# A batch's softmax weights applied by one VectorE product instead of four scalings, in both cross attentions

## The chip, the cores and the metric

The kernel runs on one core of one Trainium2 chip. The metric is the device time of one execution in microseconds (us), the median of several runs.

## The reference

A two-layer perceiver-like block on x of shape 32 batches x 32 tokens x 512. Each layer is a cross attention to a context (32 x 257 x 128), then a self attention, then a feed-forward stage (dense in layer 0, mixture of experts in layer 1). The change touches the two cross attentions alone (L0x and L1x in the program's names). Cut to the part that matters, one of them computes

```python
q_r = jnp.einsum('bshq,hqr->bhsr', q_big, W_qr)
k_r = jnp.einsum('bld,hdr->bhlr', kv_rope, W_kr)
scores = jnp.einsum('bhsr,bhlr->bhsl', q_r, k_r)
attn = jax.nn.softmax(scores, axis=-1)
ctx_c = jnp.einsum('bhsl,bld->bhsd', attn, kv_rope)
ctx_lat = jnp.einsum('bhsd,hkd->bshk', ctx_c, w_kc_kv)
out = ctx_lat.reshape(b, s, H * K) @ Wo.T
```

for 16 heads. The softmax goes over 257 context rows; the kernel subtracts the last context row from all others beforehand, so that 256 scores remain and the last one's exponent is a term of its own (the "tail").

## The kernel before, in words

Work is cut by batch. A batch has 32 tokens x 16 heads = 512 query rows, which stand as 4 groups of 128 partitions with 256 scores each. So a batch's exponents are one tile `prob` of 128 x (4 x 256) floats, of which three are used in turn. The order on every engine is written out by hand: `tensor_attention`, `scalar_attention`, `vector_attention` and `pool_attention` are loops over b, and each engine works through its own loop in order; semaphores couple them.

In one pass of its loop each engine does the following.

- TensorE (PE): turns the keys of batch b+1 (`turn_keys`, L463, L464), scores batch b (L477), mixes batch b-3 with its probabilities (`mix`, L98), turns the probabilities of batch b-2 (`turn_probs`, L490), and from b = 7 on projects a quarter of a token tile out (`project_out`, L98). For b below 7 it folds one head's output weights instead (L455).
- ScalarE (ACT): four exponentials of batch b, one for each group, which also write their sums (L573), and the tail's (L575); then the high parts of the turned probabilities of b-2 (L537), the mixed context of b-3 (L553), the high part of a projection's operand (L549), the next keys (L563).
- VectorE (DVE): the low part of a projection's operand (`split_lo`, L618), the row maxima of batch b (`find_peak`, L627, L630), then `weigh` for batch b-1, the low parts of the turned probabilities of b-2 (L595). After every fourth projection it adds the finished tile to x (L606) and takes its statistics (L149, L151, L153).
- GpSimd (POOL): rotates the context rows of batch b+2 (`rotate_keys`, L415, L418, L419, L421, L423), splits those of b-2 into high and low parts (L399, L401). After every fourth projection it stands in its queue at the root of the variance of that tile (`next_root`, L159), which waits for DVE's statistics.

`weigh` adds the tail to the four sums (L635), takes the reciprocals (L637), and then scales the four groups of `prob` in place, each by its own column of reciprocals (L640). `turn_probs` on PE waits until the sixth step of the batch is counted.

What follows `weigh` in DVE's queue is L595; what waits for its result is `turn_probs` one pass later.

Of the kernel before, what the change touches and what calls it, by code (L numbers as in the profile page):

```python
# [7 lines left out]
ALU = mybir.AluOpType  # L8
# [6 lines left out]
P = 128  # L15
BANK = 512
B, S, D = 32, 32, 512
# [5 lines left out]
LC = (L - 1) // P  # L23
# [49 lines left out]
class Signals:  # L73
# [5 lines left out]
    def take(self, name, total):  # L79
        if name not in self.sems:  # L80
            self.sems[name] = self.ctx.enter_context(self.nc.semaphore(f"s_{name}"))
        base = self.total.get(name, 0)
        self.total[name] = base + total
        return Signal(self.sems[name], base)
# [151 lines left out]
class LatentAttention(Stage):  # L236
# [15 lines left out]
    def sb(self, n, shape, dt=F32, arena=None):  # L252
        return (arena or self.arena).enter_context(self.sh.nc.sbuf_tensor(f"{self.name}_{n}", shape, dt))
# [5 lines left out]
    def attention_memory(self):  # L259
        sb, take, sh = self.sb, self.take, self.sh  # L260
        self.craw = [sb(f"craw{i}", [P, 3, DC]) for i in range(2)]
        self.rot = sb("rot", [P, 3, DC])
        self.kcos, self.ksin = sb("kcos", [P, 3, DC]), sb("ksin", [P, 3, DC])
        self.kv = [sb(f"kv{i}", [P, 3, DC]) for i in range(5)]
        self.kvT = [sb(f"kvT{i}", [P, LC * P + S]) for i in range(self.NKT)]
        self.prob = [sb(f"prob{i}", [P, 4, LC * P]) for i in range(3)]
        self.pT = [tuple(sb(f"pT_{v}{i}", [P, LC, BANK], F32R) for v in ("hi", "lo")) for i in range(2)]
        self.kvs = [tuple(sb(f"kvs_{v}{i}", [P, LC, DC], F32R) for v in ("hi", "lo")) for i in range(2)]
        self.small = [sb(f"small4_{i}", [P, 5, 4]) for i in range(4)]
        self.wn = tuple(sb(f"wn_{v}", [P, XH, D], F32R) for v in ("hi", "lo"))  # L270

        self.part_hi = [sb(f"part_hi{i}", [P, BANK], F32R) for i in range(2)]
        self.s_bank = [sh.psum(i) for i in range(3)]
        self.o_bank, self.t_bank, self.c_bank, self.k_bank = sh.psum(3), sh.psum(4, 2), sh.psum(6), sh.psum(7)
        self.c_landed = [take(f"c_landed{i}", 48 * B // 2) for i in range(2)]
        self.tabs_landed = take("rope_landed", 32)
        self.folded = take("folded", XH)
        self.wn_hi, self.wn_lo = take("wn_set", XH), take("norm_sum", XH)
        self.q_back = take("expert_landed2", 16 * self.HALF)
        self.part_hi_set, self.part_lo_set = take("copied", BPT * NT), take("squared", BPT * NT)  # L280
        self.rope = take("rope", 5 * B)
        self.kT_made = take("kT_made", B)
        self.kT_set = take("kT_set", B)
        self.scored = take("scored", 2 * B)
        self.peak = take("peak", 3 * B)
        self.exped = take("exped", 5 * B)
        self.weighed = take("weighed", 6 * B)
        self.prob_turned = take("prob_turned", 2 * B)
        self.pT_hi = take("pT_hi", 2 * B)
        self.pT_lo = take("pT_lo", 2 * B)  # L290
        self.kv_split = take("kv_split", 2 * B)
        self.mixed = take("mixed", B)
        self.ctx_set = take("ctx_set", B)
        self.projected = take("projected", BPT * NT)
        self.x_set = take("x_set", NT)
        self.ends = [(self.x_set, NT)]

        self.mixed_all = [(self.x_set, NT - 1), (self.ctx_set, B), (self.kT_set, B)]
        self.out_w = [sh.add_weights(sh.d[f"{self.name}_out"][n], OUT_HEADS * OUT_PACK, [(self.folded, OUT_HEADS * (n + 1))])
                      for n in range(XH // OUT_HEADS)]  # L300
# [180 lines left out]
    def turn_probs(self, pe, b):  # L481
        src = self.prob[b % 3]
        if b == 0:
            self.folds_kept(pe, self.FIRST)
        pe.wait_ge(self.weighed, 6 * b + 6)
        pe.wait_ge(self.pT_hi, 2 * b)
        pe.wait_ge(self.pT_lo, 2 * b)
        for c in range(LC):
            for r in range(4):
                ins = pe.e.transpose(self.t_bank[:, c * BANK + r * P:c * BANK + (r + 1) * P], src[:, r, c * P:(c + 1) * P],  # L490
                                     self.sh.ident[:])
            ins.then_inc(self.prob_turned.sem, 1)
# [128 lines left out]
    def find_peak(self, dve, b):  # L621
        mx, neg = (self.small[b % 4][:, n, :] for n in range(2))
        for g in range(2):
            bank = self.s_bank[(2 * b + g) % 3]
            dve.wait_ge(self.scored, 2 * b + g + 1)
            dve.wait_ge(self.weighed, 6 * (b - 3))
            dve.e.tensor_reduce(mx[:, 2 * g:2 * g + 2], bank.rearrange("p (r n) -> p r n", r=2), AX_X,  # L627
                                ALU.max).then_inc(self.peak.sem, 1)
        dve.wait_ge(self.peak, 3 * b + 2)
        dve.e.tensor_scalar(neg, mx, -1.0, 0.0, ALU.mult, ALU.min).then_inc(self.peak.sem, 1)  # L630

    def weigh(self, dve, b):
        dst, (sums, tail, rec) = self.prob[b % 3], (self.small[b % 4][:, n, :] for n in (2, 3, 4))
        dve.wait_ge(self.exped, 5 * b + 5)
        dve.e.tensor_tensor(sums, sums, tail, ALU.add).then_inc(self.weighed.sem, 1)  # L635
        dve.wait_ge(self.weighed, 6 * b + 1)
        dve.e.reciprocal(rec, sums).then_inc(self.weighed.sem, 1)  # L637
        dve.wait_ge(self.weighed, 6 * b + 2)
        for r in range(4):
            dve.e.tensor_scalar(dst[:, r, :], dst[:, r, :], rec[:, r:r + 1], None, ALU.mult).then_inc(self.weighed.sem, 1)  # L640


class FoldedQueries(LatentAttention):
# [2455 lines left out]
```

## Time and profile before

| | |
|---|---|
| median of 3 runs | 2112.19 us |
| lowest and highest | 2111.12, 2112.3 us |
| span of the profiled execution (first to last instruction) | 2106.8 us |
| PE busy | 1996.1 us (95%) |
| DVE busy | 1203.5 us (57%) |
| POOL busy | 972.1 us (46%) |
| mean granted TensorE clock | 0.985 |

The profiled execution's own device time isn't given beside its span; the median's 2112.19 us stands 5.4 us above the span. The first cross attention's loop over batches lies between about 125 and 385 us of the span, the second's between about 1114 and 1380 us. PE's matmuls are pipelined and their ends are modelled: a row's duration overlaps the next one's start, so gaps in the starts say more than durations.

### The profile page before, as it was taken

To read this page: it belongs to the slowest core of one execution; us is meant where nothing else is said; L and a number is where in the kernel's file an instruction comes from. 1 tells how busy PE (TensorE), PEld (TensorE's weight loads), DVE (VectorE), ACT (ScalarE), POOL (GpSimd) and SP (SyncE) were. 2 spreads that over 40 slices of the span, in tenths; PEclk is the share of its full clock that TensorE was granted. 3 is DMA by queue.
4 is the path that set the end of the run, shared out by engine and by line. 5 is a ranking of instruction groups with operands and counts; after the bars stand their busy time and mean duration, and the time that the engine had idled before them with its cause. 6 is when DMAs were issued, how large, how long until landed. Compare 5 with 4: busy or idle time off the path is not lost. (4 is left out here: it accounts for less than half of the span.)

```text
span 2106.8 us, 28714 instructions
## 1 busy us (share of the span) xinstructions
PE 1996.1 (95%) x9018; PEld 1421.9 (67%) x9018; DVE 1203.5 (57%) x2739; ACT 898.1 (43%) x2115; POOL 972.1 (46%) x928
## 2 busy tenths in 40 slices
PE   7989999998999999999998999979978999999997
PEld 6868888776688744666656888767655555555553
DVE  4368998567551022555547899779863443444444
ACT  2356666334422100333335666635524444454542
POOL 1266684211352100676768666476203444555552
PEclk9999999999999999999999999989988999999999
DMA  5421221200311100111222121110345999989887
GB/s 209 150 100 42 58 58 37 82 1 1 120 42 52 35 1 0 52 57 61 70 107 66 43 67 43 66 67 1 110 148 154 312 298 327 210 213 221 209 218 186
DMA packets 103411, 226.29 MB, mean 107 GB/s; under 512 B 14288, under 2 KB 56784, under 8 KB 94768
## 3 DMA queue, kind: packets, MB, share of 16 engines
q1 hardware_dynamic: 80688, 170.85, 24.0%
q0 software_dynamic: 21136, 51.11, 11.9%
q10 hardware_dynamic: 1440, 2.49, 0.3%
q8 instruction: 77, 1.26, 0.2%
q14 instruction: 70, 0.57, 0.1%
HBM read 266.86 MB, written 42.48 MB: 147 GB/s over the span
## 5 line engine op out<-in xcount | busy, mean ns | idle before, releaser
L98 PE MATMUL banks<-L1f_w,L1f_xT 128*128 x760 | 265.1, 492 | 1.9 <-issue 1.3
L2872 POOL DMA_INDIRECT moe_sums<-L1f_y,L1f_row x94 | 149.3, 1589 | 219.5 <-DVE L1f_is_who L2739 162.2
L159 POOL TENSOR_TENSOR rstd<-rstd,power 128x1 f32<-128x1 f32 x48 | 35.4, 738 | 361.1 <-DVE rstd L153 361.1
L98 PEld LDWEIGHTS banks<-L1f_w,L1f_xT 128*128 128x128 f32 x760 | 138.0, 192 | 82.0 <-issue 6.8
L2690 DVE SCALAR_TENSOR_TENSOR L1f_z<-banks,L1f_share,L1f_sg 128x192 f32<-128x192 f32 x95 | 39.7, 418 | 147.8 <-ACT L1f_sg L2623 147.7
L2880 POOL DMA_INDIRECT L1f_xg<-moe_rows,L1f_row x95 | 94.2, 991 | 61.5 <-DVE L1f_spare L2730 24.6
L2623 ACT ACTIVATE L1f_sg<-banks 128x192 f32<-128x192 f32 x95 | 31.4, 331 | 206.9 <-PE banks L98 145.5
L98 PE MATMUL banks<-L0f_down,L0f_z 128*128 128x512 f32 x256 | 111.1, 592 | 1.5 <-DVE L0f_z L2147 1.5
L98 PE MATMUL banks<-L0f_hT_hi,L0f_ug_hi 128*128 128x512 f32 x256 | 100.0, 391 | 0.0
L98 PE MATMUL banks<-L0f_hT_hi,L0f_ug_lo 128*128 128x512 f32 x256 | 99.6, 389 | 0.0
L98 PE MATMUL banks<-L0f_hT_lo,L0f_ug_hi 128*128 128x512 f32 x256 | 99.6, 389 | 0.0
L2600 PE MATMUL banks<-L1f_w,L1f_zT 128*128 x190 | 97.3, 594 | 1.8 <-ACT L1f_zT L2632 1.8
L2601 PE MATMUL banks<-L1f_w,L1f_zT 128*128 x190 | 97.0, 592 | 0.0
L2219 POOL TENSOR_TENSOR L0f_ug_lo<-w,L0f_ug_hi 128x512 fp32r<-128x512 f32 x32 | 42.9, 1353 | 113.2 <-ACT L0f_ug_hi L2123 113.2
L573 ACT ACTIVATE L1x_prob<-banks,L1x_small 128x256 f32<-128x256 f32 x128 | 59.0, 473 | 82.3 <-DVE L1x_small L630 82.3
L573 ACT ACTIVATE L0x_prob<-banks,L0x_small 128x256 f32<-128x256 f32 x128 | 59.0, 473 | 80.7 <-DVE L0x_small L630 80.7
L1115 PE MATMUL banks<-L1x_y,L1x_u 128*128 128x512 f32 x192 | 87.7, 593 | 1.6 <-ACT L1x_u L1165 0.9
L98 PEld LDWEIGHTS banks<-L0f_down,L0f_z 128*128 128x128 f32 x256 | 48.1, 190 | 59.7 <-issue 59.7
L2729 DVE TENSOR_SCALAR L1f_row_f<-L1f_found 128x1 f32<-128x1 f32 x95 | 14.6, 154 | 128.6 <-ACT L1f_sign L2664 127.3
L2147 DVE SCALAR_TENSOR_TENSOR L0f_z<-banks,L0f_su,L0f_sg 128x1024 f32<-128x1024 f32 x16 | 20.5, 1283 | 109.8 <-PE banks L98 109.8
L1242 POOL TENSOR_TENSOR xn<-xn,L1x_sinq 128x512 f32<-128x512 f32 x32 | 41.6, 1299 | 76.0 <-ACT xn L1141 76.0
L1246 POOL TENSOR_TENSOR L1x_y<-L1x_y,L1x_turn_part 128x1024 f32<-128x1024 f32 x32 | 75.7, 2365 | 0.0
(425 smaller groups left out, 5672.5 us busy)
## 6 DMA issues: line engine op xcount, KB each, us to landing
L1f_w<-in_experts SPq DMA_DIRECT2D x95, 1280.0 KB
L1f_laid<-moe_counts SPq DMA_DIRECT2D x59, 512.0 KB
w<-in_L1x_heads SPq DMA_DIRECT2D x16, 704.0 KB, 4.1
w<-in_L0x_heads SPq DMA_DIRECT2D x8, 1216.0 KB, 5.7
w<-in_wug SPq DMA_DIRECT2D x8, 1024.0 KB, 4.9
L0x_craw<-in_ctx SPq DMA_DIRECT2D x96, 64.0 KB, 2.9
L1x_craw<-in_ctx SPq DMA_DIRECT2D x96, 64.0 KB, 2.2
w<-in_L0x_out SPq DMA_DIRECT2D x4, 1280.0 KB, 5.5
```

What stands on the lines that cost most here:

```text
L98: ins = pe.e.matmul(out, w, m, start=first and n == 0, stop=last and n == len(pairs) - 1)
L159: pool.e.tensor_tensor(self.rstd[:, i:i + 1], self.rstd[:, i:i + 1], self.power[:, 0:1], ALU.pow).then_inc(self.rstd_set.sem, 1)
L573: act.e.activation(dst[:, r, :], bank[:, (r % 2) * 256:(r % 2 + 1) * 256], ACT.Exp, bias=neg[:, r:r + 1], accum_out=sums[:, r:r + 1]).then ...
L1115: ins = pe.e.matmul(self.sh.psum(self.SMALL), self.u[h % 2][:, c, :], self.y[k % 3][:, c, :], start=c == 0, stop=c == QC - 1)
L1242: pool.e.tensor_tensor(self.by_tile(buf[:], 1), self.by_tile(buf[:], 1), self.table(self.sinq[:, 2:3], 1), ALU.mult).then_inc(self.rest_si ...
L1246: pool.e.tensor_tensor(y[:, 0:2], y[:, 0:2], self.turn_part[k % 2][:], ALU.add).then_inc(self.pair_set.sem, 1)
L2219: pool.e.tensor_tensor(lo[:], self.ug_source(n), hi[:], ALU.subtract).then_inc(self.ug_lo.sem, 1)
L2600: pe.e.matmul(out, zT[:, 0, :], self.weights(slot, self.GU, at), start=True, stop=False)
L2601: pe.e.matmul(out, zT[:, 1, :], self.weights(slot, at, at + D), start=False, stop=True).then_inc(self.y_made.sem, 1)
L2690: dve.e.scalar_tensor_tensor(out=self.z[j % 2][:], in0=self.gu_bank(j)[:, EI:2 * EI], scalar=self.share[:, j:j + 1], in1=self.sg[j % 2][:] ...
L2872: pool.e.indirect_dma_start(self.sums[j % 2][:, :], bass.IndirectOffsetOnAxis(ap=self.row[:, j:j + 1], axis=0), self.y[j % self.NY][:], No ...
L2880: pool.e.indirect_dma_start(self.xg[j % self.NX][:], None, self.rows_of[:, :], bass.IndirectOffsetOnAxis(ap=self.row[:, j:j + 1], axis=0)) ...
```

## The change

The four scalings become one product of the whole tile with the four reciprocals, each repeated 256 times by a stride of zero. The semaphore `weighed` counts three steps a batch instead of six.

```diff
-        self.weighed = take("weighed", 6 * B)
+        self.weighed = take("weighed", 3 * B)
@@ turn_probs
-        pe.wait_ge(self.weighed, 6 * b + 6)
+        pe.wait_ge(self.weighed, 3 * b + 3)
@@ find_peak
-            dve.wait_ge(self.weighed, 6 * (b - 3))
+            dve.wait_ge(self.weighed, 3 * (b - 3))
@@ weigh
         dve.wait_ge(self.exped, 5 * b + 5)
         dve.e.tensor_tensor(sums, sums, tail, ALU.add).then_inc(self.weighed.sem, 1)
-        dve.wait_ge(self.weighed, 6 * b + 1)
+        dve.wait_ge(self.weighed, 3 * b + 1)
         dve.e.reciprocal(rec, sums).then_inc(self.weighed.sem, 1)
-        dve.wait_ge(self.weighed, 6 * b + 2)
-        for r in range(4):
-            dve.e.tensor_scalar(dst[:, r, :], dst[:, r, :], rec[:, r:r + 1], None, ALU.mult).then_inc(self.weighed.sem, 1)
+        dve.wait_ge(self.weighed, 3 * b + 2)
+        dve.e.tensor_tensor(dst[:], dst[:], rec.rearrange("p (r o) -> p r o", o=1).to_broadcast([P, 4, LC * P]),
+                            ALU.mult).then_inc(self.weighed.sem, 1)
```

## Rows read from the trace of the kernel before

**Rows 1.** The page's first part: busy us, share of the span and instructions of each engine.

```profile
PE 1996.1 (95%) x9018; PEld 1421.9 (67%) x9018; DVE 1203.5 (57%) x2739; ACT 898.1 (43%) x2115; POOL 972.1 (46%) x928
```

**Rows 2.** Busy time by stretch: length, PE, PEld, DVE, ACT, POOL, clock, DMA share, GB/s.

```profile
200.00:300.00 100.00, 99.85 (x486) 84.97 (x486) 91.58 (x171) 63.42 (x182) 73.90 (x97) 1.00 0.27 70
...
1200.00:1300.00 100.00, 99.85 (x489) 84.80 (x488) 90.40 (x168) 63.27 (x182) 73.42 (x98) 1.00 0.23 60
```

**Rows 3.** Timeline of PE: start us, us, engine, line. One L464 for each batch.

```profile
251.59 0.24 PE L464 MATMUL banks<-ident,L0x_kv 32*128 32x32 f32 x1
...
259.23 0.24 PE L464 MATMUL banks<-ident,L0x_kv 32*128 32x32 f32 x1
...
267.19 0.24 PE L464 MATMUL banks<-ident,L0x_kv 32*128 32x32 f32 x1
```

**Rows 4.** Timelines of DVE, POOL and PEld after the first tile's last projection.

```profile
198.26 0.69 DVE L606 TENSOR_TENSOR x<-x,banks 128x512 f32<-128x512 f32 x1 [0.28 <-PE banks L98]
...
200.16 0.92 POOL L159 TENSOR_TENSOR rstd<-rstd,power 128x1 f32<-128x1 f32 x1 [11.90 <-DVE rstd L153]
...
202.04 0.59 POOL L418 TENSOR_TENSOR L0x_rot<-L0x_craw,L0x_ksin 128x192 f32<-128x192 f32 x1
...
202.42 2.89 DVE L640 TENSOR_SCALAR L0x_prob<-L0x_prob,L0x_small 128x256 f32<-128x256 f32 x4
...
202.59 0.64 POOL L419 TENSOR_TENSOR L0x_rot<-L0x_craw,L0x_ksin 128x192 f32<-128x192 f32 x1
...
203.31 1.02 POOL L421 TENSOR_TENSOR L0x_kv<-L0x_kv,L0x_rot 128x384 f32<-128x384 f32 x1
...
204.41 0.74 POOL L423 TENSOR_TENSOR L0x_kv<-L0x_kv 128x256 f32<-128x256 f32 x1
...
205.44 0.37 PEld L463 LDWEIGHTS banks<-ident,L0x_kv 128*128 128x128 f32 x2
```

**Rows 5.** Timelines of DVE and PEld at the second and third tile's end.

```profile
229.09 0.68 DVE L606 TENSOR_TENSOR x<-x,banks 128x512 f32<-128x512 f32 x1
...
236.01 0.20 PEld L463 LDWEIGHTS banks<-ident,L0x_kv 128*128 128x128 f32 x2 [0.21 <-POOL L0x_kv L423]
...
259.90 0.68 DVE L606 TENSOR_TENSOR x<-x,banks 128x512 f32<-128x512 f32 x1
...
266.82 0.20 PEld L463 LDWEIGHTS banks<-ident,L0x_kv 128*128 128x128 f32 x2 [0.57 <-POOL L0x_kv L423]
```

**Rows 6.** Timelines of DVE and POOL, where a DVE operation on two SBUF tiles meets POOL's.

```profile
245.47 1.00 POOL L421 TENSOR_TENSOR L0x_kv<-L0x_kv,L0x_rot 128x384 f32<-128x384 f32 x1
...
245.57 1.44 DVE L618 TENSOR_TENSOR L0x_ctx_lo<-L0x_qT,L0x_part_hi 128x512 fp32r<-128x512 f32 x1 [0.73 <-ACT L0x_part_hi L549]
...
246.55 1.06 POOL L423 TENSOR_TENSOR L0x_kv<-L0x_kv 128x256 f32<-128x256 f32 x1
...
1320.12 1.36 DVE L618 TENSOR_TENSOR L1x_ctx_lo<-L1x_qT,L1x_part_hi 128x512 fp32r<-128x512 f32 x1 [0.20 <-ACT L1x_part_hi L549]
...
1320.89 1.05 POOL L418 TENSOR_TENSOR L1x_rot<-L1x_craw,L1x_ksin 128x192 f32<-128x192 f32 x1
```

**Rows 7.** Groups by line and shape: busy us, mean ns | idle before.

```profile
L640 DVE TENSOR_SCALAR L0x_prob<-L0x_prob,L0x_small 128x256 f32<-128x256 f32 x128 | 70.5, 612 | 1.1
...
L1852 DVE TENSOR_TENSOR L1a_pr<-L1a_pr,L1a_tiny 128x512 f32<-128x512 f32 x8 | 5.5, 692 | 0.3
...
L1474 DVE TENSOR_TENSOR L0a_wq_lo<-w,L0a_wq_hi 128x2048 fp32r<-128x2048 f32 x1 | 2.3, 2284 | 0.0
```

**Rows 8.** One line's instructions: duration ns min/median/max, first and last start.

```profile
L423 POOL TENSOR_TENSOR L0x_kv<-L0x_kv x32: 724/737/1072, 61.8 to 338.2; 128x256 f32<-128x256 f32 x32
```

**Rows 9.** Timelines of DVE and PE, at the loop's start and at its end.

```profile
139.83 1.14 DVE L640 TENSOR_SCALAR L0x_prob<-L0x_prob,L0x_small 128x256 f32<-128x256 f32 x4
...
173.05 3.26 DVE L640 TENSOR_SCALAR L0x_prob<-L0x_prob,L0x_small 128x256 f32<-128x256 f32 x4
...
359.04 0.49 PE L98 MATMUL banks<-L0x_pT_hi,L0x_kvs_hi 128*128 128x512 f32 x1 [1.50 <-ACT L0x_qT L553]
```

## The prediction

> **What bounds the kernel now.** I read the page's busy shares first: PE has 95% of the span, DVE 57%, POOL 46% [rows 1]. That says where to look, not what a change is worth, so next comes busy time by stretch. In the two cross attentions PE is busy 99.85 of 100 us while DVE has 91.58 and 90.40 and POOL about 74 [rows 2]. The reader should see two things there: PE sets the pace, and DVE is close enough behind it that it could be a bound for a batch here and there. Third is the timeline of PE, with one L464 as a mark for each batch. From batch 8 on the marks stand 7.60 us apart, nearly without exception; the exception is a batch of 7.96 us (259.23 to 267.19, after 7.64 us from 251.59 to 259.23) [rows 3]. There are three batches of 7.96 us that start so, one in the first attention and two in the second. Each is the batch behind a finished token tile. So outside a few places PE's own work is the time, and the question becomes what PE waits for at those places.
>
> The answer is in the timelines of the other engines there. After every fourth projection DVE adds the tile to x (L606) and takes statistics, POOL stands idle for them (11.90 us at the first tile), takes the root (L159) and only then rotates the next keys, L415 to L423, and PE's next key turn (L463) waits for L423 [rows 4]. From L606's start at 198.26 to L423's end at 205.15 are 6.89 us; PE needs the keys at 205.44. So 0.29 us are left when L606 starts as soon as PE has finished the tile. When DVE comes late with L606 the keys are late: the second tile's L606 is at 229.09 where PE's rhythm (198.26 + 4 x 7.60 = 228.66) would have allowed 228.66, and the load waits 0.21 us, which PE's array doesn't feel (its period stays at 7.61); the third's is at 259.90, 0.8 us late, the load waits 0.57 us and the batch costs 0.36 us [rows 3, 5]. This happens five times in each attention (the sixth tile's end comes when no keys are left to rotate), ten in all; three cost 0.36 us, the others 0 to 0.02, 1.1 us together. **This chain DVE, POOL, PE is the only place in the steady part where something other than PE sets the time, and the change touches both of its engines.**
>
> **The change on DVE alone.** It removes four L640 a batch and adds one product. The four took 4 x 612 = 2448 ns of busy time on average, 64 batches, 157 us for both attentions [rows 7]. But undisturbed, four start and end within 1.14 us [rows 9]: they overlap in part, and the mean is made of waits. The trace has no product of 1024 columns from two SBUF tiles. Between a product with a repeated column on 512 columns at 692 ns and a difference of 2048 at 2284 ns [rows 7] lies (2284 - 692) / 1536 = 1.036 ns a column, so 692 + 512 x 1.036 = 1222 ns. Undisturbed, then, the new form is 0.08 us slower than the old one, not faster. From both sides: 1.14 us (nothing lost against four) to 2.28 us (as the row of twice the size).
>
> The Trainium skill, "VectorE: DVE Perf Modes", section "The perf-mode tier table", speaks against this change in the same way: a float32 scaling within SBUF runs at two elements a cycle, a product of two tensors at one. By its errata table (58 cycles + columns per mode at 0.96 GHz) four scalings would be 775 ns and the product 1127 ns, an estimate from that page, 0.35 us worse a batch; the rows above say 0.08. Neither sum needs it.
>
> **What the waits are.** DVE's L618, a difference of two SBUF tiles on 512 columns, starts at 245.57 within POOL's L421 (to 246.47) and ends at 247.01, that is 0.54 us behind L421's end; 512 columns at 1.036 ns are 0.53. So it stood until POOL's operation was over and then ran. POOL's next, L423, starts at 246.55 and takes 1.06 us where its usual is 0.74 [rows 6, 8]; it ends 0.60 us behind L618. The same at 1320: L618 ends at 1321.48, POOL's L418 takes 1.05 instead of 0.59 [rows 4, 6]. Operations of DVE and POOL that need the same way into SBUF exclude each other, one whole operation at a time, and the turn passes at the end of each. How the four scalings live with that shows at a tile's end: 202.42 to 205.31, 2.89 us for four, one in each gap between L418, L419, L421 and L423, and POOL loses next to nothing (0.64 instead of 0.59, 0.02 on L421) [rows 4].
>
> **The change where it matters: a tile's end.** The new product is issued at 202.42 like the first scaling. It gets the way when L418 ends at 202.63, holds it for 1024 x 1.036 = 1.06 us and ends at about 203.7. Then L419 runs: behind L618 the 192-column L418 ended 0.46 us after it (1321.94 against 1321.48) [rows 6], so L419 ends at 204.2 instead of 203.23. L421 and L423 follow without further loss, so L423 ends 0.94 us later than now (0.97 less the few hundredths that the scalings cost). PE's load comes 0.94 - 0.29 + 0.05 = 0.70 us late, of which 0.18 are hidden as rows 5 show (0.54 late cost 0.36). **Cost 0.52 us for each tile's end**, when L606 comes as early as PE allows. It should: a tile's end that costs PE something gives DVE and ACT that time to catch up (after the 0.36 us at 267 the next L606, at 289.88, again waited for PE), and DVE is freer. Ten ends: +5.2, less the 1.1 that they cost today: **+4.1 us**. Bounds: from 0 new (POOL held as little as by the scalings; -1.1) to 0.52 + 0.41 us at each (L606 as late as it is today, by 0.41 us on the mean of the ten: 9.3 - 1.1 = +8.2).
>
> **In the other batches of the steady part** DVE gets 4 scalings' 2.2 to 3.2 us down to 1.1 to 2.1 (own time and the rest of one POOL operation, at most 1.0). Hidden: PE has no wait there. POOL is held up to 1.06 us once a batch, of which it has room: 7.60 us a batch against 5.7 of work. The batch behind a tile's end is the tightest, 2.1 us between L423's end at 210.96 and PE's need at 213.04; two holds make 1.9, PE's own 0.5 comes to the good. I take 0.
>
> **At the loop's start.** For b = 3 to 6 the batches go round a ring DVE maxima, ACT exponentials, ACT L537, DVE L595, in which `weigh` isn't: nothing changes. In the batch at 173.05 the four take 3.26 us [rows 9] and L595 starts late behind them; PE's batch is 7.94 there instead of 7.60, in both attentions. The product would end by 175.2 and free L595, but POOL, itself held by the product of the batch before, delays L618 and the maxima. Between -0.34 and 0 each; I take -0.2, twice.
>
> **At the loop's end** PE waits 1.50 us for the mixed context (359.04) [rows 9], 1.46 in the second attention. That chain runs over ACT from the maxima of the last batches, which DVE could start up to 0.3 us earlier. I take -0.15, twice.
>
> The rest moves as it is: no transfer, no other wait of `weighed` is near (`turn_probs` comes a pass later).
>
> **Sum:** 4.1 - 0.4 - 0.3 = +3.4 us. On the span that is 2110.2 us; with the 5.4 us around it, which the median of the runs has over this span, **2115.6 us**. A measurement of this kernel tells 0.2%, 4.2 us, from no change; so this forecast is "no change", a little on the slow side.
>
> **Rivals.**
> 1. *Slower clearly: the hold is paid in full.* POOL's hold delays L618 and L630 in turn, so that L606 stays as late as now, and each tile's end pays 0.93 us, or the batch behind it pays as well. For it: L618 and L630 wait for POOL today (1.36 instead of 0.68 us), and POOL's slack behind a tile's end is 2.1 us. Against: PE's wait gives all others time. Price 8.2 - 0.7 = +7.5: 2119.7 us. It decides as soon as L606 starts more than 0.4 us behind PE's last projection.
> 2. *POOL isn't held.* The product reads one tile and a repeated column; if that leaves POOL its way, or POOL gets in between, only the relief of DVE stays: -1.1 for the tiles' ends, -0.7 and -0.6 for start and end: 2109.8 us. For it: no row has a repeated column beside POOL. Against: L618 in both directions.
> 3. *DVE is the hidden bound.* Its 91% and the coupling over ACT in the loop's first seven batches and at its end (PE waits of 1.0, 1.2, 0.9 and 0.4 us there, 1.5 at the end) could all shrink by half, 3 us in each attention: 2106.2 us. Against: the waits before L595 there end with ACT.
>
> **How the numbers follow.** Forecast 0.45, rival 1 0.25, rival 2 0.2, rival 3 0.1. Slower by over 0.2% (above 2116.4): all of rival 1 and about a quarter of the forecast, 0.36. Faster (below 2108.0): rival 3 and a little of rival 2, 0.12. Within: 0.52. The range takes rival 2's time and rival 1's: 2109.5 to 2120. The forecast's own range is 2113.5 to 2117.5, by the bounds at start and end and a tenth of a microsecond or two at each tile's end.
>
> **What the profile would show.** One L640 a batch, TENSOR_TENSOR, 1.2 us at least and up to 2.2, mean near 1.5; DVE's busy time down by about 55 to 60 us. At each of the ten tiles' ends POOL's L419 (or L418) at 1.5 us instead of 0.64, PEld L463 waiting about 0.7 us for POOL L423 instead of 0.21 or 0.57, and the period of PE's L464 at 8.1 us there. L606 led by PE at every end. Wrong if L419 stays at 0.6 us (rival 2), if the periods behind a tile's end are 8.5 us (rival 1), or if PE's waits in the first seven batches shrink (rival 3).

## The result, and the profile after

Median of 11 runs each: 2112.19 us before (2109.82 to 2115.22), 2117.12 us after (2113.95 to 2120.03). The ratio is 1.0020, 95% interval 1.0012 to 1.0029: 4.9 us slower. The two medians alone divide to 1.0023, just beyond the 0.2% that the prediction took as the smallest difference that tells; the interval lies above 1 and has 0.2% within it, so that the change costs time is clear of the noise, and that it costs more than 0.2% is not. Forecast were 2115.6 us, +3.4.

The page after, span and busy line, to be held against [rows 1]:

```profile
span 2115.2 us, 28522 instructions
PE 1999.5 (95%) x9018; PEld 1422.0 (67%) x9018; DVE 1151.2 (54%) x2547; ACT 899.5 (43%) x2115; POOL 1019.8 (48%) x928
```

DVE issues 192 instructions fewer (64 batches by three) and is busy 52.3 us less. POOL has the same 928 instructions and is busy 47.7 us *more*: an operation that is held is counted as busy. The two sums are nearly equal, and neither says yet what PE pays.

Busy time by stretch, the two stretches of [rows 2] (us, PE, PEld, DVE, ACT, POOL, clock, DMA share, GB/s):

```profile
200.00:300.00 100.00, 98.59 (x479) 83.46 (x478) 76.37 (x133) 63.62 (x182) 80.50 (x92) 1.00 0.26 68
1200.00:1300.00 100.00, 98.28 (x477) 82.96 (x476) 75.73 (x129) 63.35 (x182) 83.94 (x96) 1.00 0.22 59
```

DVE falls from 91 to 76 of 100 us, and PE, which sets the time, falls too, from 99.85 to 98.59 and 98.28. PE loses that at the ends of the token tiles. The timeline of PE where [rows 3] stood; after one ordinary period of 7.60 us comes one of 8.13 us behind the finished tile:

```profile
254.85 0.24 PE L464 MATMUL banks<-ident,L0x_kv 32*128 32x32 f32 x1
262.45 0.24 PE L464 MATMUL banks<-ident,L0x_kv 32*128 32x32 f32 x1
270.58 0.24 PE L464 MATMUL banks<-ident,L0x_kv 32*128 32x32 f32 x1
```

Before that, at the first tile's end, the timelines of DVE, POOL and PEld, for [rows 4]:

```profile
200.49 0.68 DVE L606 TENSOR_TENSOR x<-x,banks 128x512 f32<-128x512 f32 x1
...
202.38 0.93 POOL L159 TENSOR_TENSOR rstd<-rstd,power 128x1 f32<-128x1 f32 x1 [12.37 <-DVE rstd L153]
...
204.25 0.59 POOL L418 TENSOR_TENSOR L0x_rot<-L0x_craw,L0x_ksin 128x192 f32<-128x192 f32 x1
...
204.63 1.30 DVE L639 TENSOR_TENSOR L0x_prob<-L0x_prob,L0x_small 128x1024 f32<-128x1024 f32 x1
...
204.81 1.58 POOL L419 TENSOR_TENSOR L0x_rot<-L0x_craw,L0x_ksin 128x192 f32<-128x192 f32 x1
206.47 1.02 POOL L421 TENSOR_TENSOR L0x_kv<-L0x_kv,L0x_rot 128x384 f32<-128x384 f32 x1
207.57 0.73 POOL L423 TENSOR_TENSOR L0x_kv<-L0x_kv 128x256 f32<-128x256 f32 x1
...
208.35 0.20 PEld L463 LDWEIGHTS banks<-ident,L0x_kv 128*128 128x128 f32 x2 [1.19 <-POOL L0x_kv L423]
```

The product is issued while L418 still runs (to 204.84) and ends at 205.93. The 192 columns of L419, 0.64 us in [rows 4], take 1.58 us and end 0.46 us behind it. L421 and L423 follow without further loss. At the second and third tile (DVE and PEld, for [rows 5]):

```profile
231.41 0.69 DVE L606 TENSOR_TENSOR x<-x,banks 128x512 f32<-128x512 f32 x1 [0.21 <-PE banks L98]
...
239.28 0.20 PEld L463 LDWEIGHTS banks<-ident,L0x_kv 128*128 128x128 f32 x2 [0.74 <-POOL L0x_kv L423]
...
262.34 0.69 DVE L606 TENSOR_TENSOR x<-x,banks 128x512 f32<-128x512 f32 x1 [0.22 <-PE banks L98]
...
270.21 0.20 PEld L463 LDWEIGHTS banks<-ident,L0x_kv 128*128 128x128 f32 x2 [0.74 <-POOL L0x_kv L423]
```

At these two L606 starts as soon as PE is through, and the load of the keys still waits 0.74 us for POOL, where it waited 0.21 and 0.57 us. The product as a group (line and shape: busy us, mean ns | idle before), and as one line's instructions (ns min/median/max, first and last start), for [rows 7]; below it L419's, whose maximum was 1039 ns in the first attention before:

```profile
L639 DVE TENSOR_TENSOR L1x_prob<-L1x_prob,L1x_small 128x1024 f32<-128x1024 f32 x32 | 47.8, 1493 | 1.1
L639 DVE TENSOR_TENSOR L0x_prob<-L0x_prob,L0x_small 128x1024 f32<-128x1024 f32 x32 | 46.2, 1443 | 1.1
...
L639 DVE TENSOR_TENSOR L0x_prob<-L0x_prob,L0x_small x32: 1224/1298/1899, 137.3 to 364.7; 128x1024 f32<-128x1024 f32 x32
L639 DVE TENSOR_TENSOR L1x_prob<-L1x_prob,L1x_small x32: 1224/1554/1895, 1129.0 to 1357.8; 128x1024 f32<-128x1024 f32 x32
...
L419 POOL TENSOR_TENSOR L0x_rot<-L0x_craw,L0x_ksin x32: 584/596/1584, 61.4 to 341.7; 128x192 f32<-128x192 f32 x32
```

And PE's wait at the first attention's loop end (1.50 us in [rows 9]):

```profile
363.33 0.50 PE L98 MATMUL banks<-L0x_pT_hi,L0x_kvs_hi 128*128 128x512 f32 x1 [1.31 <-ACT L0x_qT L553]
```

**The account, from PE's L464 marks.** The period of batch 8 and those of the tile ends, in us; all others from batch 8 on are 7.56 to 7.64. The last column runs from the second of the 32 marks to the last:

| kernel | attention | batch 8 | ends of tiles 1 to 5 | second to last mark |
|---|---|---|---|---|
| before | first | 7.94 | 7.60, 7.61, 7.96, 7.60, 7.61 | 216.72 |
| before | second | 7.95 | 7.60, 7.62, 7.59, 7.97, 7.96 | 219.91 |
| after | first | 7.60 | 8.59, 8.13, 8.13, 8.14, 8.13 | 219.80 |
| after | second | 8.06 | 8.59, 8.13, 8.13, 8.14, 8.13 | 222.37 |

The loops are longer by 3.08 and 2.46 us, 5.5 together. The ten tile ends cost 2 x (0.99 + 4 x 0.53) = 6.2 us instead of 1.1, so +5.1; batch 8 gives 0.34 back in the first attention and costs 0.11 in the second, -0.2. The 0.7 us that are left lie ahead of batch 8 of the first attention (the eight periods there are 48.76 us before, 49.46 after). They can't be put down to the change: two profiles of one and the same kernel, the one with the product and the late root below, have 48.39 and 49.47 us there. The loops' ends give back 0.19 and 0.15 (from 1.50 and 1.46 us of wait to 1.31 and 1.31). What the marks give to the change is 5.1 - 0.2 - 0.3 = 4.6 us, beside the 4.9 of the runs.

The two profiled spans lie 8.4 us apart, 2106.8 to 2115.2. What the loops don't explain of it: 1.4 us ahead of the first (in the first 60 us the granted clock was 0.97 against 1.00, and it is so in the later profile of a kernel with the four scalings too), some 1.8 behind the second. So one profile's span is no measure of a change of 5 us here; periods between marks in the same stretch, from batch 8 on, are. Nor do the 5.4 us between span and time that were read before the change hold in general: wherever a run's time and span are both known, they lie 1.8 to 2.5 us apart, so the profiled execution of the kernel before was a short one. The forecast doesn't rest on it, since it adds to the median.

### The profile page after: what moved, and what is told of

It is laid out like the page before. It is cut to its first block and busy times, and to the rows that moved or that the text cites. A ratio compares the mean times of both kernels' runs of the same rounds, so it can differ in the third digit from the quotient of the medians.

```text
span 2115.2 us, 28522 instructions
## 1 busy us (share of the span) xinstructions
PE 1999.5 (95%) x9018; PEld 1422.0 (67%) x9018; DVE 1151.2 (54%) x2547; ACT 899.5 (43%) x2115; POOL 1019.8 (48%) x928
```

## The experiments

Two theories. **The hold** (the prediction's): the product keeps POOL from SBUF for 1.06 us in the chain that ends in PE's key turn, where 0.29 us were free. **DVE's own time or rhythm** (the rival): the product changes how DVE, ACT and POOL fall together over the whole loop, or its length on DVE counts, and the tile's end only shows it. In all runs below, the period behind a tile's end is what decides.

**Where: the change alone at the tiles' ends, and all but there.** Twelve of the 64 batches have their product inside a tile's end, b = 10, 14, ... 30. One kernel gets the scalings back in them, the other has the product in them alone (its `four` is the negation):

```
+        if self.four(b):        # return b >= 10 and b % 4 == 2
+            for r in range(4):
+                dve.e.tensor_scalar(dst[:, r, :], dst[:, r, :], rec[:, r:r + 1], None, ALU.mult)...
+        else:
             dve.e.tensor_tensor(dst[:], dst[:], rec...to_broadcast([P, 4, LC * P]), ALU.mult)...
```

> The changed kernel, but in the one batch behind each finished token tile (b = 10, 14, 18, 22, 26, 30; twelve batches of 64) the four scalings are back. My theory (the product holds GpSimd back in the chain add to x, statistics, root, key rotation, key turn, and only there does it cost): the ten periods of TensorE behind a tile's end go from 8.59 and 8.13 us back to 7.60 to 7.96, some 5 to 6 us less than the changed kernel, 0 to 1.5 us less than the kernel before (2110.7 to 2112.2 us). Rival (the product's lateness costs everywhere, or the difference has nothing to do with the tiles' ends): it stays at 2115 to 2117 us, since 52 of 64 batches still have the product.

> The reverse: the four scalings everywhere but in the batches behind a finished token tile (twelve of 64), which have the product. My theory: nearly the whole loss stands here, periods of 8.1 to 8.6 us behind each of the ten tiles' ends, 4 to 6 us over the kernel before. Rival: 12 of 64 batches carry 12/64 of the loss, under 1 us.

Measured, the scalings at the tiles' ends and the product in the other 52 batches: 2113.02 us, ratio 1.0006 (0.9997 to 1.0015), no loss that can be told, though 0.8 us above what was expected at most; the kernel before had 2111.48 us beside it, as it had for the next three. The product in 12 batches alone: 2115.90 us, ratio 1.0021 (1.0010 to 1.0031), the whole loss of the full change (1.0020). Its ten tile ends all take 8.13 or 8.14 us, 10 x 0.53 = 5.3 us. The timelines of POOL, DVE and PEld at its second tile:

```profile
235.51 1.30 DVE L643 TENSOR_TENSOR L0x_prob<-L0x_prob,L0x_small 128x1024 f32<-128x1024 f32 x1
...
235.69 1.58 POOL L419 TENSOR_TENSOR L0x_rot<-L0x_craw,L0x_ksin 128x192 f32<-128x192 f32 x1
...
239.24 0.20 PEld L463 LDWEIGHTS banks<-ident,L0x_kv 128*128 128x128 f32 x2 [0.74 <-POOL L0x_kv L423]
```

So the place is shown. A part of what was expected of the first kernel missed: seven of its ten tile ends came back to 7.60 to 7.70 us, three stayed at 8.05 to 8.12, dearer than any tile end of before. POOL isn't held there, but L606 is late:

```profile
231.82 0.68 DVE L606 TENSOR_TENSOR x<-x,banks 128x512 f32<-128x512 f32 x1
...
235.95 2.89 DVE L641 TENSOR_SCALAR L0x_prob<-L0x_prob,L0x_small 128x256 f32<-128x256 f32 x4
...
236.13 0.65 POOL L419 TENSOR_TENSOR L0x_rot<-L0x_craw,L0x_ksin 128x192 f32<-128x192 f32 x1
...
238.74 0.20 PEld L463 LDWEIGHTS banks<-ident,L0x_kv 128*128 128x128 f32 x2 [0.72 <-POOL L0x_kv L423]
```

The batch's mark is at 230.99, so L606 starts 0.83 us behind it; in the kernel after, L606 follows PE's last projection, and it is the hold that costs. Where a tile's end costs PE nothing, DVE and ACT get no time back, and L606 may drift; no run tested this reading. That the rhythm of the other batches can make L606 late (0.76 to 0.83 us behind the mark at these three, up to 0.68 in the kernel before) is the part of the rival that is true, worth 0.45 to 0.52 us a time here.

**What takes its place when the chain has room.** POOL takes the root first and rotates the next keys behind it. Here it rotates first, with the product and with the scalings:

```
     rotate_keys(pool, b + 2)
+    o = b - 1 - self.LAG_VALUES - BPT
+    if o >= 0 and o % BPT == BPT - 1:
+        self.next_root(pool, o // BPT)
...
-            if o >= 0 and o % BPT == BPT - 1:
-                self.next_root(pool, o // BPT)
+        self.next_root(pool, NT - 1)
```

> The changed kernel, with GpSimd's root of the variance moved behind the next batch's key rotation, so that GpSimd doesn't stand idle for VectorE's statistics with the keys unrotated. My theory: the keys are early by several us, TensorE's periods behind a tile's end are 7.60 us, 6 us less than the changed kernel: about 2111 us, 0.5 to 1.5 us under the kernel before. Rival (VectorE and not GpSimd makes the keys late, or GpSimd is short of time altogether): the periods stay above 7.9 us.

> The kernel before with the same move of the root. My theory: the three periods of 7.96 us become 7.60 us, 1.1 us less than before, 2111 us, and no difference from the changed kernel with the move beyond 1 us: with GpSimd out of the chain it doesn't matter which form weighs. Rival: the scalings stay 4 to 5 us ahead of the product with the move too.

Measured: with the product 2110.31 us, ratio 0.9994 (0.9985 to 1.0003); with the scalings 2111.84 us, ratio 0.9999 (0.9990 to 1.0008). In both all ten tile ends take 7.60 us. The marks of PE around the second tile, product and late root (the edit moves L464 to L466, L463 to L465 and L423 to L425):

```profile
221.75 0.24 PE L466 MATMUL banks<-ident,L0x_kv 32*128 32x32 f32 x1
229.35 0.24 PE L466 MATMUL banks<-ident,L0x_kv 32*128 32x32 f32 x1
236.95 0.24 PE L466 MATMUL banks<-ident,L0x_kv 32*128 32x32 f32 x1
```

and POOL and DVE there:

```profile
228.70 0.74 POOL L425 TENSOR_TENSOR L0x_kv<-L0x_kv 128x256 f32<-128x256 f32 x1
...
231.80 0.93 POOL L159 TENSOR_TENSOR rstd<-rstd,power 128x1 f32<-128x1 f32 x1 [2.36 <-DVE rstd L153]
...
234.22 1.22 DVE L641 TENSOR_TENSOR L0x_prob<-L0x_prob,L0x_small 128x1024 f32<-128x1024 f32 x1
```

The keys are ready (L425, to 229.44) 2.36 us before the root can start, and the product meets no rotation. The product of the batch before does meet one: L423 there, L421 in the other kernels, starts at 226.73 and takes 1.89 us in place of 1.02, and even so the keys are early. The product costs nothing then: between this kernel and the changed one stand only the order of POOL's work and 1.0020 against 0.9994. With the scalings the same order can save at most the 1.1 us that the tile ends cost before, too little for a run to tell. The two late-root kernels lie 1.5 us apart, more than the 1 us that was expected, but their intervals overlap.

**By how much: one more hold, and as much time without a hold.** Behind the product, in the 12 batches, DVE gets one operation more on 512 columns: once with two SBUF inputs, once a reduction with one.

```
+        dve.e.tensor_tensor(dst[:, 0:2, :], dst[:, 0:2, :], dst[:, 0:2, :], ALU.max)
```

or

```
+        dve.e.tensor_reduce(self.small[b % 4][:, 0, 0:2], dst[:, 0:2, :], AX_X, ALU.max)
```

> The changed kernel plus, in the batch behind each finished token tile (b = 10, 14, 18, 22, 26, 30), one more VectorE operation on two SBUF tiles right behind the product: the maximum of half the tile with itself, 128x512, in place, 0.53 us of way into SBUF; the values stay. My theory (whole operations of VectorE and GpSimd take turns): GpSimd's L421 or L419 is held once more by 0.33 to 0.46 us, TensorE's periods behind a tile's end go from 8.13 us to about 8.5 us, 4 us over the changed kernel: 2121 us. Rival (VectorE's lateness, not GpSimd's, makes the cost, or nothing is held): periods as in the changed kernel, or the same as in the kernel with a one-input operation in this place.

> The changed kernel plus, in the same batches and the same place, a one-input VectorE operation of about the same length: the row maxima of half the tile, 128x512 to 128x2, into a spent column. My theory: a reduction of one SBUF tile holds GpSimd up not at all, VectorE has the 0.7 us to spare before it waits for ScalarE, so the periods stay at 8.13 us and the time at that of the changed kernel, 2117 us within 1.5. Rival (VectorE's own time is what costs): periods of 8.5 us or more as with the two-input operation.

Measured beside 2112.34 us of the kernel before: with two inputs 2120.10 us (five runs), ratio 1.0045 (1.0032 to 1.0058); with the reduction 2116.71 us, ratio 1.0023 (1.0014 to 1.0032), within the noise the changed kernel's 1.0020. POOL, DVE and PEld with the second two-input operation:

```profile
235.56 1.58 POOL L419 TENSOR_TENSOR L0x_rot<-L0x_craw,L0x_ksin 128x192 f32<-128x192 f32 x1
...
236.71 0.98 DVE L643 TENSOR_TENSOR L0x_prob<-L0x_prob 128x512 f32<-128x512 f32 x1
...
237.22 1.35 POOL L421 TENSOR_TENSOR L0x_kv<-L0x_kv,L0x_rot 128x384 f32<-128x384 f32 x1
...
239.43 0.20 PEld L463 LDWEIGHTS banks<-ident,L0x_kv 128*128 128x128 f32 x2 [1.07 <-POOL L0x_kv L423]
```

and with the reduction:

```profile
233.41 1.58 POOL L419 TENSOR_TENSOR L0x_rot<-L0x_craw,L0x_ksin 128x192 f32<-128x192 f32 x1
...
234.57 0.69 DVE L643 TENSOR_REDUCE L0x_small<-L0x_prob 128x2 f32<-128x512 f32 x1
...
235.07 1.02 POOL L421 TENSOR_TENSOR L0x_kv<-L0x_kv,L0x_rot 128x384 f32<-128x384 f32 x1
...
236.96 0.20 PEld L463 LDWEIGHTS banks<-ident,L0x_kv 128*128 128x128 f32 x2 [0.75 <-POOL L0x_kv L423]
```

The second operation waits until L419 is over, then holds L421: 1.35 us instead of 1.02. The wait of the load grows by the same 0.33, and the period from 8.13 to 8.46; ten times 0.33 are 3.3 us, and the two kernels lie 3.4 us apart. The reduction keeps DVE for 0.69 us, as long as the 512-column product of [rows 7] undisturbed. It starts within L419 and ends within L421, and adds nothing to either or to the period. 0.69 us more of DVE's own time cost nothing there; 0.33 us more of hold cost PE 0.33.

**Half the hold at a time.** The product in two halves of 512 columns:

```
-        dve.e.tensor_tensor(dst[:], dst[:], rec...to_broadcast([P, 4, LC * P]), ALU.mult)
+        for r in (0, 2):
+            dve.e.tensor_tensor(dst[:, r:r + 2, :], dst[:, r:r + 2, :],
+                                rec[:, r:r + 2]...to_broadcast([P, 2, LC * P]), ALU.mult)
```

> The changed kernel with the product in two halves of 128x512. My theory (a turn passes at the end of each operation): the halves lie in two gaps between GpSimd's operations and hold them by 0.46 and 0.33 us, together 0.79 in place of 0.94: the periods behind a tile's end fall from 8.13 to about 8.0 us, 1.5 us under the changed kernel. Rival (the hold is shorter than the operation when it is short, as with the four scalings, which cost 0.05): periods back near 7.6 us.

Measured: 2114.73 us, ratio 1.0013 (1.0004 to 1.0022). POOL, DVE and PEld:

```profile
233.52 1.78 DVE L640 TENSOR_TENSOR L0x_prob<-L0x_prob,L0x_small 128x512 f32<-128x512 f32 x2
...
233.70 1.05 POOL L419 TENSOR_TENSOR L0x_rot<-L0x_craw,L0x_ksin 128x192 f32<-128x192 f32 x1
234.83 1.35 POOL L421 TENSOR_TENSOR L0x_kv<-L0x_kv,L0x_rot 128x384 f32<-128x384 f32 x1
...
237.05 0.20 PEld L463 LDWEIGHTS banks<-ident,L0x_kv 128*128 128x128 f32 x2 [0.55 <-POOL L0x_kv L423]
```

Against their undisturbed 0.59 and 1.02 us, L419 is held by 0.46 us and L421 by 0.33, 0.79 together. One product held L419 by 0.99 on the same count (1.58 us; the 0.94 of the prediction and of the expectation above is counted from the 0.64 us that L419 takes beside the scalings). The 0.20 us between them is what the period gains: the tile ends take 7.93 to 7.95 us, all ten, in place of 8.13. Halves let POOL run once between them. Batch 8, though, takes 8.35 and 8.34 us in this kernel, which nothing led one to expect. DVE there:

```profile
170.41 1.28 DVE L618 TENSOR_TENSOR L0x_ctx_lo<-L0x_qT,L0x_part_hi 128x512 fp32r<-128x512 f32 x1 [0.35 <-ACT L0x_part_hi L549]
...
172.92 1.02 DVE L630 TENSOR_SCALAR L0x_small<-L0x_small 128x4 f32<-128x4 f32 x1
```

The kernel after has 0.69 and 0.54 us for the two, and PE's next mixed context waits 0.47 us for ACT. The trace shows POOL in DVE's way here: its L423 runs from 170.40 to 171.15, and L618 ends 0.54 us behind it; its L415 runs from 172.90 to 173.92, and L630 ends 0.02 us behind it. The second attention has the same two rows (1.27 and 1.02 us). That these two make the batch longer, 8.35 us where the kernel after has 7.60, is argued from the trace; no run tested it.

**The version that could be best, again.** The same kernel as the one with the product and the late root, measured again:

> The product with the late root once more, to narrow its interval against the kernel before (0.9985 to 1.0003 in five rounds). My theory: all ten periods at 7.60 us, 1.1 us less there, 0.3 at the loop's start in the first attention; 0.5 to 1.5 us under the kernel before, ratio 0.9993 to 0.9998. Rival: above 1.0, in which case the first measurement was chance.

2111.18 us, ratio 0.9991 (0.9983 to 1.0000). Two measurements, 1.2 us each below the kernel before, and both intervals end at no change or just beyond it (1.0003 and 1.0000): faster by at most 0.2%, if at all, and slower by no more than 0.03%.

## Why the prediction was right, step by step

- **What bounds the kernel, and where**: right. Twelve batches' products, ten of them at a tile's end with keys to rotate, carry the loss (ratio 1.0021, beside 1.0020 with the product in all 64); the other 52 cost nothing that a run can tell.
- **The size of the hold**: right. Worked out was that L423 ends 0.94 us later; at the second tile L606's start to L423's end went from 6.89 us to 7.82 (231.41 to 239.23), 0.93 more. L419 1.58 us for "1.5", the shortest product 1224 ns for 1222. The Trainium skill, "VectorE: DVE Perf Modes", section "The TRN2 errata", has two figures for it. By the errata table, which the prediction gave, the product would be 1127 ns; by the formula for a float32 tensor_tensor add that stands below the table, (columns + 151) at 0.96 GHz, it is 1224 ns. The measured 1224 decides for the second.
- **0.52 us for a tile's end**: right at eight of ten, 0.53. At the two first ones it is 0.99, and there the mechanism of rival 1 holds: L606 is late, and the price is about the 0.93 us of that rival. Counted from PE's mark L606 starts 0.47 us later than in [rows 4] in the first attention, and 0.48 us later in the second (0.36 us behind the mark where it was 0.12 ahead of it). It isn't chance: the kernel with the scalings at the tiles' ends and the two with one more operation have it 0.35 to 0.37 us behind the mark too, in both attentions. The kernel with the product at the tiles' ends alone differs from the one after only in the batches ahead and between; its L606 starts 0.11 us ahead of the mark, and its first tiles take 8.13 us. So it is the products of the batches ahead of a first tile's end that make its L606 late; which of them, and over which engine, stays open. In the first attention at least, PE had just gained 0.34 us at batch 8 (7.94 to 7.60), time that DVE and ACT otherwise have to catch up; in the second there was no such gain. With the halves, where batch 8 costs PE 8.35 and 8.34 us, L606 is in time at both. This is the term that was too small: +5.1 for the ten ends instead of +4.1.
- **Loop start**: -0.34 in the first attention, +0.11 in the second, together -0.2 where -0.4 was taken. This term was about twice too large; it and the tile ends' err in the same direction.
- **Loop end**: right, 0.19 and 0.15 for 0.15 twice.
- **DVE's busy time**: 52 us less for "55 to 60", means of 1443 and 1493 ns for "near 1.5". The prediction's 157 us for the scalings was 64 x 2448 ns and counts twice where they overlap; by the groups they kept DVE busy for 70.5 and 70.0 us, and the products for 46.2 and 47.8, so 46.5 us of the saving are theirs.
- **L606 led by PE at every end**: at eight, not at the two first ones.
- **Rival 2, POOL isn't held**: fell at once; a repeated column holds POOL like a second tile. **Rival 3, DVE the hidden bound**: DVE went from 91 to 76 of 100 us, and the periods ahead of batch 8 didn't shrink (48.76 to 49.46 us and 51.55 to 51.61); the reduction, 0.69 us more on DVE in the tightest place, cost nothing either.

The likeliest class, within 0.2%, was missed by 0.7 us by the medians: 4.9 us are 0.23%. The 0.46 us by which each of the two first tiles was dearer than the other eight are together more than that. By the interval of the ratio the class isn't settled. The time itself came out 1.5 us above the forecast, inside the forecast's own range; by the marks the terms of the sum are +5.1, -0.2 and -0.3 for the +4.1, -0.4 and -0.3 that were forecast.

## What to carry to other kernels

Merging four short DVE operations into one long one can be slower although it relieves the engine that it runs on, if the long one takes a path that another engine needs in whole operations: four scalings left POOL a gap each, one product left none. Before such a change, look for the place where the two engines' work lies in the chain that PE waits for, and count the hold there, not DVE's busy time. Where the hold hurts, moving the held work ahead of the wait (here the keys before the root) took away all that the ten tile ends cost, which no form of the operation did.

## What the runs showed of the hardware

VectorE and GpSimd took turns by the whole operation. Against L419, whose undisturbed time is 0.59 us, a 1024-column product with two SBUF inputs cost GpSimd 0.99 us, a 512-column one 0.46; against L421 a 512-column one cost 0.33; four scalings of 256 columns cost 0.05 together, and the reduction with one input nothing. An inverse sum read with a repeated column counted as a full second input, which no row of before had shown. The Trainium skill, "SBUF — State Buffer", section "Who interferes with whom", says that a VectorE instruction with two SBUF inputs and a GpSimd instruction that reads SBUF exclude each other for the whole instruction, and that a reduction never contends; by that rule the traces here agree, with 0.99 us for the one and nothing for the other. The other direction is as strong: the product, 1224 ns alone, took up to 1899 ns, and four scalings that need 1.14 us alone took 2.89 [rows 4, 9]. Even a 128x4 tensor_scalar with one input (L630), 0.17 us alone, took 1.02 us beside GpSimd's L415 in the kernel with halves. GpSimd's busy time rose by 47.7 us without one instruction more, so a busy share there is not work.
